# Fused cross-attention stage: a LayerNorm shift moved from VectorE to GpSimd, and the statistics that follow it moved half a step

## The chip, the cores and the metric

One core of one Trainium2 chip runs the whole program. The metric is the device time of one execution in microseconds (us). Engines are named PE (TensorE), DVE (VectorE), ACT (ScalarE), POOL (GpSimd) and SP (the queue that issues most plain DMAs).

## The reference, cut to what matters

Two blocks follow each other on 128 x 64 = 8192 tokens of width 128, 16 heads of 8. The first is self attention, cross attention and a mixture of 8 experts (top 2), each followed by a LayerNorm. The second is a pre-norm cross attention and an MLP. The change lies where the two meet:

```python
# end of block 0 (y: tokens after cross attention)
x  = _layernorm(y + _moe(y, ...), ln3_g, ln3_b)       # third LayerNorm: scale, gain g, shift b
# start of block 1
qn = _layer_norm(x, ln1_g, ln1_b)                      # the "next" LayerNorm, of the new tokens x
Q  = (qn @ wq + bq)                                    # K, V from the context
x  = x + softmax(Q K^T / sqrt(8)) V @ wo + bo
x  = x + gelu(_layer_norm(x, ln2_g, ln2_b) @ w1 + b1) @ w2 + b2
```

## The kernel before, in words

The program runs five parts one after the other: constants, the first block's two attentions, the routing, the experts (their output rows go to DRAM), and `fused_phase` with the final MLP behind it. Only `fused_phase` (L1280) is touched.

`fused_phase` works on 16 groups of 512 tokens (a tile of 128 partitions x 4 x 128). Every engine has its own queue, and its order is written out by hand in a function `step(a)` of that engine; step g works on several groups at once. With g as the group whose attention is in hand (two "quads" of scores, 2g and 2g+1, each as two halves):

- POOL (L1881), step g: `front_rstd(g+2)` (L1865: four tiny instructions that make the reciprocal deviation and the bias of two LayerNorms at once, the own one of group g+2 and the next one of group g+1), the last three of the eight indirect fetches of the expert rows of group g+3 (`fetch`, L1857), `spread(2g-2)` (L1827), `fetch_open(g+4)`, `add_bias(g-1)` (L1834), three fetches of g+4, `spread(2g-1)`, two more fetches of g+4.
- DVE (L1781), step g: `subtract`, `weigh_first(g+3)` (L1720), `maximum`, `recip(2g-1)` (L1685), `weigh_second(g+3)` (L1729), `subtract`, `own_statistics(g+3)` (L1749), `normalise(g-1)` (L1691), `front_moments(g+3)` (L1765), two `maximum` and two `subtract` of quad 2g+2, `recip(2g)`, `gain_own(g+3)` (L1738), `residual(g-1)`, `shift_own(g+3)` (L1743), `maximum`, `next_statistics(g+3)` (L1756), `normalise(g)`.
- ACT (L1636), step g: among exponents and copies, `scale_own(g+2)` (L1615, makes z3) and `scale_next(g+1)` (L1621, makes z4); both wait for `fnb_ready` of POOL.
- PE (L1497): the matmuls and transposes of attention, with `turn_z(g+1)` (L1491), `widen` (L1458, waits for `spread`) and `values` (L1436).

`front_moments(g+3)` aggregates the statistics of the own LayerNorm of group g+3 (written by `own_statistics(g+3)`) together with those of the next LayerNorm of group g+2 (written by `next_statistics(g+2)`), and one semaphore, `fmv_ready`, hands both to POOL. In the kernel before, `next_statistics(g+3)` stands near the end of step g and is used in step g+1. The new tokens `held(a)` lie in `x3`, which has a place for every group. `shift_own` waits for `zg3_ready`, `next_statistics` for `x3_ready`; POOL's `add_bias` also waits for `x3_ready` of a group four steps older than the one made in that step.

The fetches exist for groups up to 15, so POOL issues five of them in steps up to 11 and three up to 12; the first steps (-4 to -1) only fill the pipeline.

Of the kernel before, what the change touches and what calls it, by code (L numbers as in the profile page):

```python
# [7 lines left out]
ALU = mybir.AluOpType  # L8
# [3 lines left out]
P = 128  # L12
D = 128
# [6 lines left out]
GP = GT // P  # L20
# [1259 lines left out]
def fused_phase(nc, c, r, tag, layer, x2_src, rows, final):  # L1280
# [5 lines left out]
    with ExitStack() as ctx:  # L1286
# [33 lines left out]
        zg3 = n.sb("zg3", [P, 2, GP, D])  # L1320
# [28 lines left out]
        def held(a):  # L1349
            return x3[:, bass.ds(a.place, 1)].rearrange("p o t d -> p (o t) d")  # L1350
# [7 lines left out]
        with nc.Block() as block:  # L1358
# [311 lines left out]
            def _(dve):  # L1670
# [20 lines left out]
                def normalise(a, h):  # L1691
                    quad = a.g * 2 + h
                    dve.wait_ge(r_ready, quad + 1)
                    if beyond(a.g, 0):
                        dve.wait_ge(o_ready, a.g)
                    dve.wait_ge(ov_ready, quad + 1)
                    dve.tensor_tensor(ot[:, GT // 2 * h:GT // 2 * h + GT // 2], ps_o[:, GT // 2:GT], ov[:, h, :],
                                      ALU.mult).then_inc(ot_ready, 1)
# [41 lines left out]
                    dve.tensor_tensor(zg3[:, a.u], z3[:, a.u], c.row["ln3_g"][:, None, :].broadcast_to([P, GP, D]),  # L1740
                                      ALU.mult).then_inc(zg3_ready, 1)

                def shift_own(a):  # L1743

                    dve.wait_ge(zg3_ready, a.g + 1)
                    dve.tensor_tensor(held(a), zg3[:, a.u], c.row["ln3_b"][:, None, :].broadcast_to([P, GP, D]),  # L1746
                                      ALU.add).then_inc(x3_ready, 1)

                def own_statistics(a):  # L1749

                    dve.wait_ge(fy_ready, a.g + 1)
# [29 lines left out]
                def step(a):  # L1781
                    if a.unrolled and a.g == NG:
                        final.dve_part(dve, True)
                    g = a.g
                    if a.exists():
                        subtract(g * 2 + 1, 0)
                    if a.shift(3).exists():
                        weigh_first(a.shift(3))
                    if a.exists():
                        maximum(g * 2 + 1, 1)  # L1790
                    if a.shift(-1).exists():
                        recip(g * 2 - 1, 1)
                    if a.shift(3).exists():
                        weigh_second(a.shift(3))
                    if a.exists():
                        subtract(g * 2 + 1, 1)
                    if a.shift(3).exists():
                        own_statistics(a.shift(3))
                    if a.shift(-1).exists():
                        normalise(a.shift(-1), 1)  # L1800
                    if a.shift(3).exists() or a.shift(2).exists():
                        front_moments(a.shift(3))
                    if a.shift(1).exists():
                        maximum(g * 2 + 2, 0)
                        maximum(g * 2 + 2, 1)
                        subtract(g * 2 + 2, 0)
                        subtract(g * 2 + 2, 1)
                    if a.exists():
                        recip(g * 2, 0)
                    if a.shift(3).exists():  # L1810
                        gain_own(a.shift(3))
                    if a.shift(-1).exists():
                        residual(a.shift(-1))
                    if a.shift(3).exists():
                        shift_own(a.shift(3))
                    if a.shift(1).exists():
                        maximum(g * 2 + 3, 0)
                    if a.shift(3).exists():
                        next_statistics(a.shift(3))
                    if a.exists():  # L1820
                        normalise(a, 0)
                over_steps(dve, step, NG - 4)
# [3 lines left out]
            def _(pool):  # L1826
# [30 lines left out]
                def fetch(a, first, end):  # L1857
                    for i in range(first, end):
# [3 lines left out]
                            in_offset=bass.IndirectOffsetOnAxis(ap=sl[:, a.u, choice, t:t + 1], axis=0)).then_inc(  # L1862
                                yg_in[a.u], 16)

                def front_rstd(a):  # L1865
                    pool.wait_ge(fmv_ready, a.g + 1)
                    if beyond(a.g, 1):
                        pool.wait_ge(z3_ready, a.g - 1)
                    if beyond(a.g, 2):
                        pool.wait_ge(fz_ready, a.g - 2)  # L1870
                    pool.tensor_tensor(fneg[:, a.u, :], fmv[:, a.u, :, 0], c.minus_one[:, 0:2 * GP], ALU.mult)
                    pool.tensor_tensor(frstd[:, a.u, :], fmv[:, a.u, :, 1], c.eps[:, 0:2 * GP],
                                       ALU.add).then_inc(fvar_ready, 1)
                    pool.wait_ge(fvar_ready, a.g + 1)
                    pool.tensor_tensor(frstd[:, a.u, :], frstd[:, a.u, :], c.minus_half[:, 0:2 * GP],  # L1875
                                       ALU.pow).then_inc(frstd_ready, 1)
                    pool.wait_ge(frstd_ready, a.g + 1)
                    pool.tensor_tensor(fnb[:, a.u, :], fneg[:, a.u, :], frstd[:, a.u, :], ALU.mult).then_inc(
                        fnb_ready, 1)

                def step(a):  # L1881
# [18 lines left out]
                        spread(g * 2 - 1, 1)  # L1900
                    if a.shift(4).exists():
                        fetch(a.shift(4), 3, 4)
                        fetch(a.shift(4), 4, 5)
                pool.wait_ge(bob_ready, 1)
                over_steps(pool, step, NG - 4)
# [502 lines left out]
```

## Time and profile before

| | us |
|---|---|
| median of 3 runs | 1475.5 |
| lowest and highest | 1467.96 and 1479.77 |
| span of the profiled execution, first to last instruction | 1416.2 |
| median less that span (what lies around it) | 59.3 |
| fused stage in the profile, from the first fetch to the last residual add | about 949 to 1284 |

The profiled execution has no separate time of its own, so the median less the span is taken for what lies around the span. Times in rows are us from the span's start. Instruction durations overlap a little at their edges; what counts in a queue is the distance from one start to the next.

### The profile page before, as it was taken

Reading aid. Unit: us, or ns where it says so; the run is one execution under the profiler, and the core shown is the slowest. Engines: PE = TensorE matmul, PEld = TensorE weight load, DVE = VectorE, ACT = ScalarE, POOL = GpSimd, SP = SyncE. Lnnn points to the kernel's source line nnn. Section 1 sums busy time; section 2 is a strip of 40 time slices with the busy share of each in tenths; the row PEclk is TensorE's granted clock in tenths of the full one; section 3 lists DMA queues with packets and bytes.
Section 4 is the critical chain, followed back from the end, with each engine's and each line's share of the span. In section 5 each row is a group of like instructions: output and inputs, shape, how many; then the busy total and the mean of one; then the engine's idle time right before and its main releaser. Section 6 shows DMA issues by size and latency. Waiting matters only on the chain. (4 is left out here: it accounts for less than half of the span.)

```text
span 1416.2 us, 59902 instructions
## 1 busy us (share of the span) xinstructions
PE 1253.1 (88%) x23136; PEld 1052.9 (74%) x23136; DVE 962.8 (68%) x2123; ACT 993.5 (70%) x2030; POOL 866.3 (61%) x1340
## 2 busy tenths in 40 slices
PE   4999999989999998668899999961699999998997
PEld 2778877777888887657899999960577777785775
DVE  3777777767787875588455555534799999963331
ACT  1777777767888885298566666641789999974553
POOL 1567667666766774310899999848677777423331
PEclk9999999999999998559899999985799999999999
DMA  3233323323232242052222222222233333121221
GB/s 108 70 94 93 111 90 96 99 85 91 82 89 81 81 129 76 8 183 70 61 67 69 68 67 70 65 62 65 76 90 92 92 94 91 52 61 53 71 70 45
DMA packets 140281, 113.91 MB, mean 80 GB/s; under 512 B 17184, under 2 KB 113952, under 8 KB 140192
## 3 DMA queue, kind: packets, MB, share of 16 engines
q1 hardware_dynamic: 131744, 95.42, 22.9%
q0 software_dynamic: 8448, 17.32, 4.9%
q8 instruction: 54, 0.88, 0.3%
q14 instruction: 35, 0.29, 0.1%
HBM read 78.55 MB, written 34.08 MB: 80 GB/s over the span
## 5 line engine op out<-in xcount | busy, mean ns | idle before, releaser
L832 DVE TENSOR_REDUCE at_mx<-at_ps_s 128x16 f32<-128x1024 f32 x128 | 156.1, 1220 | 106.8 <-PE at_ps_s L561 60.7
L761 ACT ACTIVATE at_pt<-at_ps_t 128x1024 f32<-128x1024 f32 x128 | 130.6, 1020 | 56.3 <-PE at_ps_t L575 55.4
L2225 POOL DMA_INDIRECT ex_xg<-x,ex_ti x136 | 148.0, 1088 | 23.3 <-issue 21.9
L754 ACT ACTIVATE at_pr<-at_dd 128x1024 f32<-128x1024 f32 x128 | 135.2, 1056 | 34.7 <-DVE at_dd L840 34.6
L2306 DVE COPY ex_wt<-experts 128x1156 f32 x136 | 104.8, 772 | 75.7 <-DVE ex_y L2312 72.9
L2285 ACT ACTIVATE ex_hg<-ex_ps_h,ex_wt 128x128 f32<-128x128 f32 x544 | 154.4, 372 | 1.3 <-PE ex_ps_y L2254 1.2
L840 DVE TENSOR_TENSOR at_dd<-at_ps_s,at_mx 128x1024 f32<-128x1024 f32 x128 | 153.7, 1202 | 0.1
L1860 POOL DMA_INDIRECT l_yg<-rows,l_sl x128 | 128.9, 1007 | 33.8 <-issue 30.5
L2245 PE MATMUL ex_ps_h<-ex_xt,ex_wt 128*128 128x128 f32 x1088 | 147.2, 279 | 0.0
L575 PE MATMUL at_ps_t<-ident,at_pr 128*128 128x128 f32 x1024 | 139.9, 280 | 5.2 <-issue 4.2
L2254 PE MATMUL ex_ps_y<-ex_wt,ex_hg 128*128 128x128 f32 x1088 | 143.7, 275 | 0.7 <-ACT ex_hg L2285 0.7
L962 POOL TENSOR_TENSOR at_rcx<-at_rc,own 128x256 f32<-128x256 f32 x64 | 39.2, 613 | 159.9 <-DVE at_rc L848 159.9
L2245 PEld LDWEIGHTS ex_ps_h<-ex_xt,ex_wt 128*128 128x128 f32 x1088 | 133.3, 193 | 2.7
L2254 PEld LDWEIGHTS ex_ps_y<-ex_wt,ex_hg 128*128 128x128 f32 x1088 | 132.3, 192 | 1.1 <-ACT ex_hg L2285 1.1
L575 PEld LDWEIGHTS at_ps_t<-ident,at_pr 128*128 128x128 f32 x1024 | 113.5, 142 | 23.2 <-issue 15.3
L589 PE MATMUL at_ps_o<-at_pt,vx 128*32 128x64 f32 x4096 | 123.7, 222 | 5.3 <-issue 3.4
L594 PE MATMUL at_ps_o<-at_pt,count 128*32 128x64 f32 x4096 | 122.6, 221 | 6.3 <-issue 6.2
L589 PEld LDWEIGHTS at_ps_o<-at_pt,vx 128*32 128x32 f32 x4096 | 95.5, 111 | 32.8 <-ACT at_pt L761 22.0
L594 PEld LDWEIGHTS at_ps_o<-at_pt,count 128*32 128x32 f32 x4096 | 97.8, 111 | 7.0 <-issue 7.0
L2277 ACT ACTIVATE ex_xt<-ex_ps_x 128x128 f32<-128x128 f32 x136 | 37.7, 277 | 91.8 <-PE ex_ps_x L2237 82.6
L1130 PEld LDWEIGHTS l_ps_s<-mlp_w,mlp_hid 128*128 128x128 f32 x512 | 67.1, 191 | 31.7 <-issue 29.6
L953 POOL TENSOR_TENSOR at_qb<-at_qt,side 128x256 f32<-128x256 f32 x128 | 74.5, 613 | 24.7 <-ACT at_qt L734 19.1
(240 smaller groups left out, 3174.9 us busy)
## 6 DMA issues: line engine op xcount, KB each, us to landing
rows<-ex_y SPq DMA_DIRECT2D x136, 64.0 KB
x<-at_ln_out SPq DMA_DIRECT2D x32, 256.0 KB, 3.2
at_kx<-in_xt SPq DMA_DIRECT2D x16, 256.0 KB, 2.8
at_qx<-in_xt SPq DMA_DIRECT2D x16, 256.0 KB, 2.8
at_vin<-in_xt SPq DMA_DIRECT2D x16, 256.0 KB, 2.7
at_xr<-in_x SPq DMA_DIRECT2D x16, 256.0 KB, 2.9
x1t<-at_xt SPq DMA_DIRECT2D x16, 256.0 KB, 3.3
at_kx<-in_ctxt SPq DMA_DIRECT2D x16, 256.0 KB, 2.8
```

What stands on the lines that cost most here:

```text
L575: tr = pe.transpose(ps_t[:, b, r, :], pr[:, p, r, 2 * b:2 * b + 2, :], c.ident[:, :])
L589: pe.matmul(ps_o[32 * r:32 * r + 32, SEQ * b:SEQ * b + SEQ], c.vx[:, 0, QB * h + b, r, 24 * f:24 * f + 32], pt[:, 2 * h + b // 2, b % 2, r ...
L594: mm = pe.matmul(ps_o[32 * r:32 * r + 32, GT // 2:GT // 2 + SEQ], c.count[:, b, f, :], pt[:, 2 * h + b // 2, b % 2, r, SEQ * f:SEQ * f + SEQ],
L754: act.activation(pr[:, p], dd[:, p], ACT.Exp, scale=SCALE).then_inc(p_ready, 1)
L761: act.activation(pt[:, 2 * h + p], ps_t[:, :, :, :], ACT.Copy).then_inc(pt_ready, 1)
L832: dve.tensor_reduce(mx[:, p], ps_s[:, :, 4 * p:4 * p + 4, :], AX.X, ALU.max).then_inc(mx_ready, 1)
L840: dve.tensor_tensor(dd[:, p], ps_s[:, :, 4 * p:4 * p + 4, :], mx[:, p, :, :, None].broadcast_to([P, 4, 4, SEQ]), ALU.subtract).then_inc(d_ ...
L1860: pool.indirect_dma_start(out=yg[:, a.u, choice, t, :], out_offset=None, in_=rows, in_offset=bass.IndirectOffsetOnAxis(ap=sl[:, a.u, choic ...
L2225: pool.indirect_dma_start(out=xg[:, s, :], out_offset=None, in_=x_src, in_offset=bass.IndirectOffsetOnAxis(ap=ti[:, s:s + 1], axis=0)).the ...
L2245: mm = pe.matmul(ps_h[s % HB][:, f, :], wt[:, s % HB, W1 + P * f:W1 + P * f + P], xt[:, s % HB, :], start=True, stop=True)
L2254: mm = pe.matmul(ps_y[s % 2][:, :], hg[:, s % 2, f, :], wt[:, s % HB, W2 + D * f:W2 + D * f + D], start=(f == 0), stop=(f == FC - 1))
L2285: ins = act.activation(hg[:, s % 2, f, :], ps_h[s % HB][:, f, :], ACT.Gelu, bias=wt[:, s % HB, B1 + f:B1 + f + 1])
```

## The change

`shift_own` becomes a POOL instruction. It stands in POOL's step g, for group g+2, between the fourth and the fifth fetch of group g+4. `next_statistics` moves on DVE from the end of step g (for group g+3) to the middle of step g+1, directly before `front_moments`, and so, written for step g, works on group g+2.

```diff
 DVE, functions
-                def shift_own(a):
-
-                    dve.wait_ge(zg3_ready, a.g + 1)
-                    dve.tensor_tensor(held(a), zg3[:, a.u], c.row["ln3_b"][:, None, :].broadcast_to([P, GP, D]),
-                                      ALU.add).then_inc(x3_ready, 1)
-
 DVE, step
                     if a.shift(-1).exists():
                         normalise(a.shift(-1), 1)
+                    if a.shift(2).exists():
+                        next_statistics(a.shift(2))
                     if a.shift(3).exists() or a.shift(2).exists():
                         front_moments(a.shift(3))
...
                     if a.shift(-1).exists():
                         residual(a.shift(-1))
-                    if a.shift(3).exists():
-                        shift_own(a.shift(3))
                     if a.shift(1).exists():
                         maximum(g * 2 + 3, 0)
-                    if a.shift(3).exists():
-                        next_statistics(a.shift(3))
                     if a.exists():
                         normalise(a, 0)
 POOL, functions
+                def shift_own(a):
+
+                    pool.wait_ge(zg3_ready, a.g + 1)
+                    pool.tensor_tensor(held(a), zg3[:, a.u], c.row["ln3_b"][:, None, :].broadcast_to([P, GP, D]),
+                                      ALU.add).then_inc(x3_ready, 1)
 POOL, step
                         spread(g * 2 - 1, 1)
                     if a.shift(4).exists():
                         fetch(a.shift(4), 3, 4)
+                    if a.shift(2).exists():
+                        shift_own(a.shift(2))
+                    if a.shift(4).exists():
                         fetch(a.shift(4), 4, 5)
```

## Rows read from the trace of the kernel before

**Rows 1.** Busy us by stretch: length, then PE, PEld, DVE, ACT, POOL, clock, DMA

```profile
1031.40:1205.00 173.60, 160.09 (x4041) 128.36 (x4042) 172.83 (x410) 157.96 (x252) 136.53 (x170) 1.00 0.34 91
1205.00:1222.30 17.30, 15.91 (x405) 12.76 (x406) 17.20 (x41) 15.73 (x26) 8.37 (x10) 1.00 0.21 59
1222.30:1237.80 15.50, 14.14 (x357) 11.10 (x359) 14.68 (x25) 14.05 (x23) 5.01 (x7) 1.00 0.17 49
```

**Rows 2.** Timeline of POOL, one steady step; start, us, operation, [idle time before it]

```profile
1118.23 0.20 POOL L1871 TENSOR_TENSOR l_fneg<-l_fmv,minus_one 128x8 f32<-128x8 f32 x1 [1.12 <-DVE l_fmv L1778]
...
1123.39 1.14 POOL L1860 DMA_INDIRECT l_yg<-rows,l_sl  x1 [0.30 <-DVE l_rc L1689]
1124.56 1.01 POOL L1831 TENSOR_TENSOR l_rcx<-l_rc,own 128x256 f32<-128x256 f32 x1
...
1125.95 1.28 POOL L1838 TENSOR_TENSOR l_xb<-l_x,l_bob 128x512 f32<-128x512 f32 x1
...
1131.29 0.75 POOL L1831 TENSOR_TENSOR l_rcx<-l_rc,own 128x256 f32<-128x256 f32 x1 [0.22 <-DVE l_rc L1689]
1132.18 0.99 POOL L1860 DMA_INDIRECT l_yg<-rows,l_sl  x1 [0.15 <-issue]
...
1135.53 0.20 POOL L1871 TENSOR_TENSOR l_fneg<-l_fmv,minus_one 128x8 f32<-128x8 f32 x1 [1.11 <-DVE l_fmv L1778]
```

**Rows 3.** Timeline of ACT, the same step: its z4 copy, and its two waits

```profile
1125.87 0.58 ACT L1632 ACTIVATE l_qx<-l_ps_g 128x512 f32<-128x512 f32 x1
...
1128.23 1.45 ACT L1570 ACTIVATE l_qb<-l_ps_g,l_side,side 128x512 f32<-128x512 f32 x2 [0.83 <-PE l_ps_g L1471]
...
1131.21 0.38 ACT L1606 ACTIVATE l_ov<-l_ps_o 128x256 f32<-128x256 f32 x1 [0.61 <-issue]
```

**Rows 4.** Timeline of DVE, the same step

```profile
1124.23 0.87 DVE L1746 TENSOR_TENSOR l_x<-l_zg,const_rows 128x512 f32 x1
1125.02 1.21 DVE L1673 TENSOR_REDUCE l_mx<-l_ps_s 128x16 f32<-128x1024 f32 x1
1126.16 0.28 DVE L1762 BATCH_NORM_STATS2 l_fstats<-l_x 128x6 f32 x1
...
1126.37 0.66 DVE L1762 BATCH_NORM_STATS2 l_fstats<-l_x 128x6 f32 x3
1126.95 0.40 DVE L1697 TENSOR_TENSOR l_ot<-l_ps_o,l_ov 128x256 f32<-128x256 f32 x1
...
1134.68 0.17 DVE L1778 BATCH_NORM_AGGREGATE l_fmv<-l_fstats 128x2 f32<-128x6 f32 x1
...
1134.77 0.54 DVE L1778 BATCH_NORM_AGGREGATE l_fmv<-l_fstats 128x2 f32<-128x6 f32 x7
```

**Rows 5.** Durations in ns (least, median, most) of three lines over the run

```profile
L1831 POOL TENSOR_TENSOR l_rcx<-l_rc,own x32: 612/744/1029, 1018.4 to 1280.1; 128x256 f32<-128x256 f32 x32
L1860 POOL DMA_INDIRECT l_yg<-rows,l_sl x128: 940/980/1341, 949.4 to 1210.2; - x128
L1746 DVE TENSOR_TENSOR l_x<-l_zg,const_rows x16: 691/873/1735, 970.8 to 1228.5; 128x512 f32<-128x512 f32 x8, 128x512 f32 x8
```

**Rows 6.** Timeline of PE: the query projection, and the key projection behind `values`

```profile
1127.09 1.02 PE L1471 MATMUL l_ps_g<-l_qx,mats 128*128 128x512 f32 x2
...
1130.10 1.12 PE L1466 MATMUL l_ps_g<-l_kx,mats 128*128 128x512 f32 x2
```

**Rows 7.** Timeline of POOL while the pipeline fills, and at its first wait

```profile
979.09 0.21 POOL L1871 TENSOR_TENSOR l_fneg<-l_fmv,minus_one 128x8 f32<-128x8 f32 x1
...
1011.90 0.20 POOL L1871 TENSOR_TENSOR l_fneg<-l_fmv,minus_one 128x8 f32<-128x8 f32 x1 [6.63 <-DVE l_fmv L1778]
```

**Rows 8.** Timeline where the shift (DVE) meets `add_bias` (POOL), last group

```profile
1228.48 1.74 DVE L1746 TENSOR_TENSOR l_x<-l_zg,const_rows 128x512 f32<-128x512 f32 x1
...
1228.40 1.27 POOL L1838 TENSOR_TENSOR l_xb<-l_x,l_bob 128x512 f32<-128x512 f32 x1
```

**Rows 9.** Timeline of POOL: the one late fetch of the ten steady steps

```profile
1181.74 0.94 POOL L1860 DMA_INDIRECT l_yg<-rows,l_sl  x1 [1.40 <-issue]
```

## The prediction, made before the changed kernel ran

> **What bounds the kernel now.** I read the busy time by stretch first, then the timelines of POOL, ACT and DVE over one step, then the chain that ended last, to see where the stage hangs outside its steady part. The fused stage runs ten steps between 1031.4 and 1205.0 (that is where POOL's `front_rstd` starts), 17.36 us each [rows 1]; an undisturbed one takes 17.30 (1118.23 to 1135.53 [rows 2]). In this stretch DVE is busy 172.8 of 173.6 us, PE 160.1, ACT 158.0 [rows 1]: DVE has no gap and sets the step. POOL's 136.5 us look light, but its queue is not. Between two fetches lie 0.30 us that nothing fills, and the only real gaps of its step are 0.22 us before the second `spread` and 1.11 before `front_rstd`, which waits for DVE's moments [rows 2]: 1.3 us of slack a step. ACT has gaps of 0.83 and 0.61 [rows 3].
>
> **What is taken from DVE.** The shift of 512 columns: from its start to the next one's, 1125.02 - 1124.23 = 0.79 us a step [rows 4]. The statistics only change place (1126.16 to 1126.95, another 0.79). DVE's own work falls to 17.3 - 0.8 = 16.5 us a step. If nothing else bound, ten steps would give back 8 us.
>
> **What is given to POOL.** One add of 128x512 with a broadcast row. POOL does the same shape in `add_bias`, 1.28 us [rows 2]. The gap of 0.30 between two fetches gives way to the smaller ones around a tensor instruction (0.03 before, 0.15 behind, as round the spreads), so POOL's step grows by 1.2 us against 1.3 of slack. By occupation alone it just fits.
>
> **What the new order closes.** `front_moments` on DVE now stands behind `next_statistics`, which waits for POOL's shift, which stands behind the second `spread` and a fetch; and POOL's next step begins with `front_rstd`, which waits for those moments. That is a loop of one step through the whole POOL queue. Its length from `front_rstd` on, in durations of before:
> - 1118.23 to 1131.07, where POOL is free for the second `spread` (1131.29 less its wait of 0.22) [rows 2]: 12.84;
> - `spread` 0.75, gap 0.15, fetch 0.99 [rows 2]: 14.7;
> - 0.05 and the shift 1.28 [rows 2]: 16.1;
> - POOL's semaphore to DVE, 0.12, an estimate between 0 and the 0.22 that DVE's takes to POOL;
> - four statistics 0.87 (1126.16 to 1127.03), 0.04, eight moments 0.63 (1134.68 to 1135.31) [rows 4]: 1.54;
> - 0.22 back to POOL (1135.31 to 1135.53) [rows 2, 4].
>
> Together 17.95 us. Off it comes what POOL loses to DVE today. The first `spread` takes 1.01 where it begins while DVE's shift runs (1124.23 to 1125.10) [rows 2, 4]; with the shift gone I take the least of its line, 0.61 [rows 5], so 0.4 off. The fetch at 1123.39 takes 1.14 [rows 2] against a median of 0.98 [rows 5]; 0.1 off. The second `spread` no longer starts right on DVE's `recip`, in `weigh_second`, because 1.6 us of DVE work (shift and statistics) leave the stretch before it; 0.1 off. That makes 17.35. DVE needs 16.5 and waits some 0.1 to 0.9 us for the shift.
>
> A second loop runs through ACT and PE. ACT's z4 copy ends 8.4 us after the moments (1126.45 less 1118.01 [rows 3]); PE's query projection and `values` take 3.0 (1127.09 to 1130.10 [rows 6]); then 0.1 and `recip` 0.6, 0.15 and `spread` 0.61, 0.15 and fetch 0.99, shift 1.33, 0.12, 1.54: 17.0. It doesn't decide, but is near. ACT gets its bias up to 1.7 us later behind DVE's `subtract`, since statistics and wait now stand between that and the moments; its gaps of 0.83 and 0.61 [rows 3] give way, as projection and `recip` come no later than before.
>
> So a steady step costs 17.35 for 17.30: ten of them +0.5 us. Bounds: 16.5 (POOL's fetches and gaps shrink beside a lighter DVE) and 17.95 (no contention is won back), so -8 and +6.5.
>
> **Filling the pipeline.** From 949 to 981 the chain that ended last runs through POOL alone: fetch after fetch, then `front_rstd`, which shows no wait before it at 979.09 [rows 7]. Step -2 now holds the shift of group 0 (1.2 us more), and behind it POOL does one fetch (1.1) while DVE needs 0.12 + 1.54 + 0.22: 0.8 of waiting. So the first z4, and with it all attention, starts 2.0 us later. Step -1 loses as much again, but there the chain runs through PE and DVE, and POOL has 6.63 us of wait at 1011.90 [rows 7]: nothing. Between 0 and +2.5, I take +2.0.
>
> **Draining it.** From step 12 on POOL is light (8.4 us busy of 17.3 [rows 1]), so the shift is early and DVE's gain shows: 0.7 us in step 12. In the next stretch the last shift took 1.74 us [rows 8], as it met `add_bias`; with it gone PE, 14.1 of 15.5 us busy [rows 1], lets about 0.8 through. Together -1.5; between 0 and -2.5.
>
> **The hiccup.** Once in the ten steps a fetch came 1.1 us late (1.40 before it, not 0.30 [rows 9]), and POOL's slack took most of it. Without slack: +0.7.
>
> **The sum.** +0.5 + 2.0 - 1.5 + 0.7 = +1.7 us on a span of 1416.2; with the 59.3 us around it 1477. The runs of before lie between 1468.0 and 1479.8, so their median of 1475.5 may itself be off by a few us.
>
> **A rule of the skill, weighed.** DVE's shift takes 691, 873 and 1735 ns (least, median, most) [rows 5]. The longest began beside `add_bias`, which ran to 1229.67, and ended 0.55 us behind it [rows 8]: it stood still while POOL ran. The Trainium skill (SBUF — State Buffer, its single rule on the shared port pair) says that a DVE instruction with two SBUF inputs and a GpSimd instruction that reads SBUF exclude each other for the whole instruction, and the one that comes second pays; by that rule, the trace agrees. It is the ground for the first rival below.
>
> **The rivals.**
> - *POOL's instructions meet DVE's two-input ones (slower).* DVE reaches `weigh_first` 1.6 us earlier than before, about 8.8 us behind the moments, which is where `add_bias` ends if `spread` is shortened; and the second `spread` still lies in `weigh_second`. If they block each other, DVE or POOL loses up to 0.6 us a step, as the shift's 0.87 to 1.74 over 0.69 shows [rows 5, 8]; it decides once it eats the 0.1 us of wait that my loop leaves DVE. With 17.95 a step: +6.5 + 2.0 - 1.5 + 0.7 = +8, 1483. With 0.6 more, 1489. For it: the pair in [rows 8]. Against it: the shift itself falls on statistics and on reads of PSUM.
> - *DVE's saving comes through (faster).* If POOL closes its loop in 16.5, the step is DVE's: -8 + 2.0 - 1.5 = -7.5, 1468. For it: DVE alone has no gap [rows 1]. Against it: the median fetch (0.98) is already near the least (0.94) [rows 5], and 0.8 would have to come from there.
> - *ACT's gaps don't give way.* Then its later bias is added, 0.8 to 1.3 us a step: +10 to +14, 1486 to 1490. Against it: what both gaps wait for comes earlier now.
>
> **How the numbers follow.** A measurement tells about 1% (15 us) from no change. Forecast (step 17.2 to 17.6): 0.60, 1475 to 1481. Meeting or contention not won back: 0.18, 1482 to 1489. ACT: 0.05. DVE's saving: 0.17, 1466 to 1472. Hardly any of these passes 15 us; with a few us of spread between runs, slower by over 1% gets 0.09, faster 0.05, within 1% 0.86. The range that leaves out 2 in 10 is 1467 to 1486.
>
> **What would show it.** Right: POOL's `front_rstd` starts 17.2 to 17.6 us apart; the gap before it is 0.6 to 0.9 us, not 1.11; DVE has a gap of 0.1 to 0.9 before `next_statistics`, released by POOL's shift; the first `spread` takes about 0.6; the z4 of group 0 is 2 us later; ACT waits for the bias, with smaller gaps elsewhere. Wrong: steps of 16.6 with DVE still gapless, a much longer `weigh_first` or `add_bias`, or ACT keeping both its gaps. A median outside 1467 to 1486 would be wrong as a whole.

## The result, and the profile after

| us | before | after | ratio, 95% interval |
|---|---|---|---|
| first set of runs (4 and 4) | 1474.3 (1468.0 to 1479.8) | 1455.9 (1452.0 to 1458.1) | 0.9873 [0.9846, 0.9900] |
| same kernel again, second set | 1474.1 | 1457.9 | 0.9880 [0.9827, 0.9932] |
| same kernel again, fifth set | 1418.7 | 1427.4 | 1.0058 [1.0035, 1.0082] |

The change made the kernel 18 us faster, where 1.7 us slower was forecast and 1467 was the lower end of the range. But the third row says that this is only half of the answer. A set here is a group of kernels that ran together on one chip, each with the kernel before beside it. In six sets the kernel before took 1474.3, 1474.1, 1474.7, 1419.0, 1418.7 and 1475.0 us: two values 56 us apart, no single run between 1428.2 and 1465.6, and always one value among the timed runs of a set. In two sets at 1474 the change gains 1.3 and 1.2%, in one at 1419 it costs 0.6%. So there are two questions: what the 56 us are, and what the change does with and without them.

The profiled execution of after, from the first set, took 1456.8 us:

```profile
core 0: 1454.1 us, clock 0.940
```

So 2.7 us lie around the span. For the kernel before, 59.3 us had been put there. A profile of the kernel before taken in the second set settles it: time 1473.8, span 1471.1, the same 2.7 us. The profile that stands ahead of the prediction was taken in an execution of the 1419 kind (span 1416.2), and the times beside it were of the 1474 kind; whether it ran together with them is not on record. The missing 55 us were not around the span. By the starts of `front_rstd` 3.3 us of them lie before the ten steady steps, 47.4 in these and 4.2 behind.

Busy us in ten steady steps, each time from one `front_rstd` to the tenth after it (columns as in [rows 1]: length, PE, PEld, DVE, ACT, POOL, clock, DMA share and GB/s): first the kernel before in a 1474 set, then after in a 1474 set, then after in a 1419 set.

```profile
1034.70:1255.70 221.00, 187.14 (x4038) 145.13 (x4038) 173.14 (x410) 161.54 (x251) 135.39 (x170) 0.95 0.26 72
```

```profile
1040.20:1241.50 201.30, 170.36 (x4044) 130.94 (x4042) 166.03 (x401) 158.79 (x251) 143.59 (x180) 1.00 0.29 79
```

```profile
1032.00:1212.60 180.60, 162.10 (x4049) 127.37 (x4052) 166.67 (x401) 158.32 (x251) 143.17 (x181) 1.00 0.32 88
```

Against [rows 1] (173.60 us) the work of DVE is nearly the same: 173 us in the kernel before in both kinds, 6 to 7 less in after, which lacks the shift. What differs is the length in which it lies: 22.1, 20.1, 18.1 and, for the kernel before in a 1419 set, 17.4 us a step. In the first row DVE idles 48 us. What it waits for stands in its timeline; after, 1474 set:

```profile
1111.00 1.22 DVE L1673 TENSOR_REDUCE l_mx<-l_ps_s 128x16 f32<-128x1024 f32 x1
1114.67 0.56 DVE L1689 RECIPROCAL l_rc<-l_ps_o 128x64 f32<-128x64 f32 x1 [2.45 <-PE l_ps_o L1452]
```

L1452 is the end of the value product `values`: 128 small pairs of weight load and matmul. Alone it takes 1.83 us. The weight loads of one such product of the kernel before in a 1474 set:

```profile
1125.85 0.16 PEld L1447 LDWEIGHTS l_ps_o<-l_pt,vx 128*32 128x32 f32 x8 [0.16 <-issue]
...
1127.84 0.12 PEld L1447 LDWEIGHTS l_ps_o<-l_pt,vx 128*32 128x32 f32 x2 [0.35 <-issue]
1128.54 0.17 PEld L1447 LDWEIGHTS l_ps_o<-l_pt,vx 128*32 128x32 f32 x4 [0.58 <-issue]
1129.30 0.11 PEld L1447 LDWEIGHTS l_ps_o<-l_pt,vx 128*32 128x32 f32 x1 [0.59 <-issue]
...
1130.02 0.18 PEld L1452 LDWEIGHTS l_ps_o<-l_pt,count 128*32 128x32 f32 x4 [0.55 <-issue]
1130.75 0.52 PEld L1487 LDWEIGHTS l_ps_g<-mats,l_ot 128*128 128x128 f32 x4 [0.55 <-issue]
```

TensorE does a few pairs, then stands still for 0.55 to 0.6 us with nothing that releases it ("issue"), and again. Beside it POOL's queue runs three fetches:

```profile
1124.70 0.20 POOL L1871 TENSOR_TENSOR l_fneg<-l_fmv,minus_one 128x8 f32<-128x8 f32 x1 [1.11 <-DVE l_fmv L1778]
...
1127.26 1.03 POOL L1860 DMA_INDIRECT l_yg<-rows,l_sl  x1 [0.16 <-issue]
1128.59 0.95 POOL L1860 DMA_INDIRECT l_yg<-rows,l_sl  x1 [0.30 <-issue]
1129.85 0.94 POOL L1860 DMA_INDIRECT l_yg<-rows,l_sl  x1 [0.31 <-issue]
```

The first gap in the loads opens 0.2 us after the first of them begins. This is what I call the standstill. Two lines measure it for the whole stage, the answers for L1452's weight loads in the profile ahead of the prediction and in the second set (idle us before its loads, times):

```profile
L1452 PEld LDWEIGHTS l_ps_o<-l_pt,count x2048: 106/110/110, 1014.2 to 1279.1; 128*32 128x32 f32 x187
...
  issue: 2.7, 2
```

```profile
L1452 PEld LDWEIGHTS l_ps_o<-l_pt,count x2048: 105/110/178, 1016.1 to 1334.9; 128*32 128x32 f32 x187
...
  issue: 24.2, 45
```

After has 15.2 us in 29 gaps in the 1474 set and 1.9 in one gap in the 1419 set. In the steady steps of the 1419 sets a product beside two or three fetches takes 1.8 to 2.1 us, in those of the 1474 sets mostly 3.0 to 6.2, and a product beside none takes 1.83 to 1.86 in both.

Which products are hit, in the 1474 sets: a step has two, `values(a,0)` about when `front_rstd` runs, and `values(a-1,1)` about when the first three fetches of g+4 run. In the kernel before the first stands still in all of the ten steady steps (3.7 to 5.8 us), the second in seven of them (2.7 to 5.3; 1.9 to 2.1 in the others). After has only the second left; its two products of one step, weight loads and POOL:

```profile
1100.29 0.16 PEld L1447 LDWEIGHTS l_ps_o<-l_pt,vx 128*32 128x32 f32 x8 [0.17 <-issue]
...
1101.94 0.19 PEld L1452 LDWEIGHTS l_ps_o<-l_pt,count 128*32 128x32 f32 x8
...
1111.84 0.11 PEld L1452 LDWEIGHTS l_ps_o<-l_pt,count 128*32 128x32 f32 x1 [0.60 <-issue]
...
1112.55 0.17 PEld L1447 LDWEIGHTS l_ps_o<-l_pt,vx 128*32 128x32 f32 x6 [0.56 <-issue]
1113.29 0.18 PEld L1452 LDWEIGHTS l_ps_o<-l_pt,count 128*32 128x32 f32 x7 [0.57 <-issue]
```

```profile
1100.35 0.21 POOL L1869 TENSOR_TENSOR l_fneg<-l_fmv,minus_one 128x8 f32<-128x8 f32 x1 [0.80 <-DVE l_fmv L1772]
...
1102.91 1.03 POOL L1852 DMA_INDIRECT l_yg<-rows,l_sl  x1 [0.16 <-issue]
...
1109.04 1.03 POOL L1852 DMA_INDIRECT l_yg<-rows,l_sl  x1
1110.38 1.00 POOL L1852 DMA_INDIRECT l_yg<-rows,l_sl  x1 [0.30 <-issue]
1111.68 0.94 POOL L1852 DMA_INDIRECT l_yg<-rows,l_sl  x1 [0.30 <-issue]
1115.39 0.74 POOL L1823 TENSOR_TENSOR l_rcx<-l_rc,own 128x256 f32<-128x256 f32 x1 [2.76 <-DVE l_rc L1689]
...
1117.29 1.29 POOL L1860 TENSOR_TENSOR l_x<-l_zg,const_rows 128x512 f32 x1
```

The first product runs from 1100.29 to 1102.12, beside `front_rstd`, and is over 0.8 us before the next fetch: with the statistics ahead of the moments, the moments, `front_rstd` and the three fetches behind it come later against PE. The second product, from 1110.09, meets the last two of three fetches (the first ended at 1110.07) and ends at 1114.38, 4.3 us for 1.8. Its last gap closes at 1113.29, 0.7 us after the last fetch has left POOL.

TensorE's granted clock has a part in it too. In the first of the three rows above it is 0.95 over the ten steps, in the other two 1.00: in the kernel before, five of the ten steps show 0.86 to 0.93, which is to say that the clock stood at the lower of its two levels (1.2 GHz for 2.4) for some of the step. A step at 1.00 and the longest one, both of the kernel before in the second set:

```profile
1056.10:1077.40 21.30, 17.81 (x410) 13.79 (x406) 17.35 (x41) 16.40 (x27) 13.56 (x18) 1.00 0.27 75
...
1099.70:1124.70 25.00, 20.96 (x420) 16.38 (x413) 17.60 (x41) 16.30 (x26) 13.46 (x18) 0.86 0.24 63
```

The five steps at 1.00 take 21.2 to 21.5 us, the five others 21.4 to 25.0, together 7.4 us more. As an estimate from these steps, up to 7.4 of the 19.7 us that the change takes off the ten steps went with the drops of the clock, and the rest with the standstill alone. In after and in stats_only, where only the second product stands still, no steady step shows a drop.

Where the 17.0 us between the spans of the two kernels went (1471.1 and 1454.1, by the starts of `front_rstd`): the ten steps -19.7, filling the pipeline +5.5 (1040.2 for 1034.7), from there to the end -2.8.

### The profile page after: what moved, and what is told of

It reads as the page before. It is cut to its first block and busy times, and to the rows that moved or that the text cites. A ratio compares the mean times of both kernels' runs of the same rounds, so it can differ in the third digit from the quotient of the medians.

```text
span 1454.1 us, 59906 instructions
## 1 busy us (share of the span) xinstructions
PE 1269.1 (87%) x23136; PEld 1059.8 (73%) x23136; DVE 951.4 (65%) x2107; ACT 995.2 (68%) x2030; POOL 878.9 (60%) x1356
## 5 line engine op out<-in xcount | busy, mean ns | idle before, releaser
L1852 POOL DMA_INDIRECT l_yg<-rows,l_sl x128 | 125.9, 983 | 31.8 <-issue 29.4
L1673 DVE TENSOR_REDUCE l_mx<-l_ps_s 128x16 f32<-128x1024 f32 x64 | 76.3, 1213 | 25.8 <-PE l_ps_s L1412 20.8
```

Of the source, the lines that this page charges most:

```text
L1852: pool.indirect_dma_start(out=yg[:, a.u, choice, t, :], out_offset=None, in_=rows, in_offset=bass.IndirectOffsetOnAxis(ap=sl[:, a.u, choic ...
```

## The experiments

The theory at the start: the gain is the statistics' place, because it lets one product a step escape the fetches. Rivals: it is DVE's relief, by the shift on POOL; or the two kernels differ for a reason that has nothing to do with the order. The kernel before beside each kernel belongs to the same set.

**Both kernels again (second set).** No edit.

> The kernel before, unchanged, profiled once more beside its own timed runs. The profile of before has a span of 1416 us under a median of 1475, that of after a span of 1454 under 1456. Theory A (the profile of before was of an execution that its timed runs are not like): the span comes out at 1465 to 1477, a steady step of the fused stage takes 20 to 21 us in place of 17.3, and TensorE stands still for about 3 us in its value products, as it does in after. Rival B (the timed runs have 59 us outside the span): span 1416 again, time 1475. Ratio to before 1.00 in both.

1475.2, ratio 1.0004 [0.9979, 1.0029]; span 1471.1.

> The kernel after, unchanged. Theory A: span about 1454, time about 1456, ratio 0.987, steps of 20.1 us with the same standstill of TensorE. Rival C (either kernel falls into the state with or without standstill by chance): one of the runs comes out near 1420.

1457.9, 0.9880 [0.9827, 0.9932]. The gain repeats, and so does the span of the kernel before: its first profile is the one that stands apart.

**The two halves of the change (second set).**

```diff
# stats_only: the statistics move, the shift stays on DVE
+                    if a.shift(2).exists():
+                        next_statistics(a.shift(2))
                     if a.shift(3).exists() or a.shift(2).exists():
                         front_moments(a.shift(3))
...
-                    if a.shift(3).exists():
-                        next_statistics(a.shift(3))
```

> Only the statistics are moved, the shift stays on VectorE. If the gain of the change lies in the shift leaving VectorE, the ratio is 1.00 (0.997 to 1.004). If it lies in where the statistics stand (they leave the stretch between the first maximum and normalise, so that normalise and the subtraction behind it come 0.8 us earlier), the ratio is 0.987 to 0.993.

1451.8, 0.9844 [0.9789, 0.9898], step 20.5: somewhat more than I had expected of it.

```diff
# shift_only: shift_own on POOL, directly behind the third fetch of its step; statistics in their old place
                         fetch(a.shift(3), 7, 8)
+                    if a.shift(2).exists():
+                        shift_own(a.shift(2))
```

> Only the shift goes to GpSimd, directly behind the third fetch of a step; the statistics stand where they stood. If the gain lies in the shift leaving VectorE, the ratio is 0.987 to 0.993, unless VectorE waits for GpSimd before the statistics (the shift ends there about 7.7 us behind the moments, VectorE comes to the statistics at 7.4, so a wait of 0.3 us). If the gain is that of the statistics' place, the ratio is 1.00 to 1.01.

1485.8, 1.0070 [1.0043, 1.0097], step 23.0. The whole gain is the move of the statistics; the shift on POOL alone, in this place, costs 0.7%. The place is not that of the change: here the shift stands ahead of the first `spread`. With both moved, as in after, the step is 0.4 us shorter than in stats_only (20.1 for 20.5), but the ten steps begin 6.7 us later (1040.2 for 1033.5), so the time is no better.

**No indirect fetch at all (third set).**

```diff
# plain_fetch: eight plain DMAs per group on SP; GpSimd's fetch does nothing
+                    for choice in range(2):
+                        for t in range(GP):
+                            sp.dma_start(yg[:, a.u, choice, t, :], rows[bass.ds(a.place * GT + (choice * GP + t) * P, P), :]).then_inc(yg_in[a.u], 16)
...
-                        pool.indirect_dma_start(
```

> The kernel before, but the expert rows come by plain DMAs of the same size from SP's queue, in order and not gathered, so GpSimd issues no fetch (the output is that of the wrong rows; everything else is computed). Theory P (TensorE's value products, 128 pairs of load and matmul, stand still wherever two or three of GpSimd's indirect fetches run beside them; 1.83 us alone, 3.7 to 5.8 beside fetches): every value product takes 1.8 to 2.0 us, the steady step is 17.0 to 17.5 us instead of 22, the time 1405 to 1425. Rival Q (the standstill is TensorE's own, from its loop or its rate, whatever GpSimd does): the products keep 3.7 to 5 us, time over 1450.

The gather is left out, so the rows are not those of the tokens, at equal bytes. 1406.2, 0.9539 [0.9513, 0.9564]. All the steady products take 1.83 to 1.86 us. `front_rstd` starts 17.1 us apart, and POOL waits for the moments:

```profile
1085.46 0.20 POOL L1869 TENSOR_TENSOR l_fneg<-l_fmv,minus_one 128x8 f32<-128x8 f32 x1 [3.43 <-DVE l_fmv L1781]
...
1102.57 0.20 POOL L1869 TENSOR_TENSOR l_fneg<-l_fmv,minus_one 128x8 f32<-128x8 f32 x1 [3.43 <-DVE l_fmv L1781]
```

The same bytes in the same stage, by plain DMAs, hold nothing up. So it is the indirect fetches on GpSimd, not the amount of their traffic. Whether it is their issue on GpSimd, the queue that they go through or the scattered rows is not separated: the plain DMAs read rows that follow each other. (Part of the time is a faster fill, as the fetches filled it.)

**GpSimd waits for the first product (third set).**

```diff
# before_wait: the kernel before with
                         front_rstd(a.shift(2))
+                    if a.shift(-1).exists():
+                        pool.wait_ge(pv_ready, g * 2 - 1)
+                        tick(0)
```

> The kernel before, only that GpSimd waits for the first value product of the step (quad 2g-2) before its three first fetches (with a tiny instruction that carries the wait). The statistics stay where they were. Theory P, by which the change gains because it starts these fetches only after that product: the products of the first quad take 1.8 us, the second ones keep 4.2, the step is 20 to 20.7 us, the time 1450 to 1460 (ratio 0.984 to 0.990). If the gain has to do with VectorE's order itself: 1470 to 1485.

1455.4, 0.9860 [0.9833, 0.9888], step 20.5, first product 1.83 us in each step, second 4.3 to 5.6, once 1.86. The granted clock over the ten steps is 0.98 for 0.95 in the kernel before of the second set. This is the test of the mechanism: DVE's order isn't touched, no work is taken away, a wait and a tiny instruction are added, and the time falls as far as with the change.

**The second product freed instead (third set).** Four fetches behind the second `spread`, one before `add_bias`.

```diff
# stats_apart (on stats_only) and before_apart (on the kernel before)
+                        fetch(a.shift(4), 0, 1)
...
                         add_bias(a.shift(-1))
-                        fetch(a.shift(4), 0, 1)
-                        fetch(a.shift(4), 1, 2)
-                        fetch(a.shift(4), 2, 3)
...
                         spread(g * 2 - 1, 1)
+                        fetch(a.shift(4), 1, 2)
+                        fetch(a.shift(4), 2, 3)
```

> Statistics moved as in the change, shift on VectorE, and GpSimd's fetches taken out of the second value product as well: in step g it does one fetch of group g+4, add_bias, the second spread and then the other four. Theory P: both value products near 1.9 us, step 17.4 to 18.2 us, time 1420 to 1432. Rival Q: 1450 or more. If the four fetches at the end of the step reach into the next first product, it is that one that takes 3 to 4 us, and the time 1435 to 1450.

1493.4, 1.0133 [1.0105, 1.0161], step 23.8.

> The same order of GpSimd's fetches on the kernel before, with the statistics in their old place. Theory P: the second product is free of fetches, the first one meets the three fetches of the next group as before where the moments come early; step 18 to 21 us, time 1430 to 1462, slower than stats_apart. Rival Q: 1470 to 1480.

1498.2, 1.0151 [1.0123, 1.0180], step 24.5. Both are misses of mine. The second product is free (1.83 to 1.86), but in the steady steps POOL of stats_apart no longer waits before `front_rstd`, and the three fetches behind that meet the first product, which runs from 1130.80 to 1136.92, 6.1 us:

```profile
1127.25 0.94 POOL L1860 DMA_INDIRECT l_yg<-rows,l_sl  x1 [0.30 <-issue]
1128.21 0.21 POOL L1871 TENSOR_TENSOR l_fneg<-l_fmv,minus_one 128x8 f32<-128x8 f32 x1
...
1130.77 1.03 POOL L1860 DMA_INDIRECT l_yg<-rows,l_sl  x1 [0.16 <-issue]
1132.11 0.96 POOL L1860 DMA_INDIRECT l_yg<-rows,l_sl  x1 [0.30 <-issue]
1133.37 0.94 POOL L1860 DMA_INDIRECT l_yg<-rows,l_sl  x1 [0.30 <-issue]
1138.01 0.84 POOL L1831 TENSOR_TENSOR l_rcx<-l_rc,own 128x256 f32<-128x256 f32 x1 [3.69 <-DVE l_rc L1689]
```

Two more things add to the loss. The four fetches now run beside the scores (L1412, 32 loads), and these stand still as well; of stats_apart:

```profile
1127.69 0.20 PEld L1412 LDWEIGHTS l_ps_s<-l_kb,l_qb 32*128 32x128 f32 x2 [0.52 <-issue]
1129.10 0.55 PEld L1412 LDWEIGHTS l_ps_s<-l_kb,l_qb 32*128 32x128 f32 x11 [1.21 <-issue]
```

In the ten steps such gaps before L1412's loads add up to 21.3 us, in the kernel before to 3.9. So it is not the value products alone that can be hit. And the granted clock is 0.86 over the ten steps of stats_apart and 0.88 over those of before_apart, for 0.95 in the kernel before.

**Both products freed (fourth set).** stats_wait is stats_only with the wait of before_wait. The two others have that wait and POOL's fetches split into two ahead of `add_bias` and three behind the second `spread`, on stats_only and on the kernel before:

```diff
# stats_two_three and before_two_three
                         fetch_open(a.shift(4))
                         fetch(a.shift(4), 0, 1)
                         fetch(a.shift(4), 1, 2)
                         add_bias(a.shift(-1))
                         spread(g * 2 - 1, 1)
                         fetch(a.shift(4), 2, 3)
                         fetch(a.shift(4), 3, 4)
                         fetch(a.shift(4), 4, 5)
```

> A control for the theory that the statistics' move gains only because it lets the first value product of a step run before GpSimd's fetches. With the statistics moved and the shift left on VectorE that product already runs free (1.83 us) in every step, so GpSimd's explicit wait for it should change nothing: 1450 to 1455 us, step 20.4 to 20.6, first product 1.83 us and second 4.5 as there. If the wait itself were what gained in the kernel before (by holding GpSimd back for some other reason), it should gain again here, about 15 us: 1435 to 1440.

1432.3 for 1419.0, 1.0086 [1.0067, 1.0106], step 18.3.

> Statistics moved, GpSimd waits for the first product, and the early fetches of group g+4 are split: two behind the first spread, then add_bias and the second spread, then three. By the standstill theory both value products of a step now run beside no fetch or only the edge of one (1.83 to 2.5 us each), and the step falls to 17.5 to 19 us, so 1415 to 1435 us. By the rival (any order in which GpSimd has more to do between the second spread and the next moments loses, as the two kernels with four fetches there did) the step is 21 to 24 us and the time 1460 to 1495. In between, 1440 to 1455: one product is still hit, and the trace says which.

1439.3 for 1419.0, 1.0116 [1.0082, 1.0149], step 19.2.

> The same wait and the same split of the fetches, with the statistics where they stood before. If the standstill beside fetches is all that separates the kernels, the place of the statistics matters no more once both products are free: same time as its companion with the statistics moved, within 5 us. If the statistics' move has a gain of its own, this one is slower by 10 us or more. And if it is below 1440, the kernel before was held up by GpSimd's order alone.

1427.2 for 1419.0, 1.0048 [1.0031, 1.0065], step 18.4.

The set was one without the standstill (the kernel before 1419.0; products beside three fetches 2.0 to 2.1 us), so what these three were made for was not tested. They showed two other things. The order that frees products costs something by itself: even stats_wait, whose wait holds nothing back here, takes 18.3 us a step, as the statistics' move alone does in the fifth set. And in before_two_three, where `add_bias` was moved beside `weigh_first`, DVE's four instructions took 2.52 us for 1.12 in the kernel before, 1.4 us more, where the step grew by 1.0; the kernel before, then DVE and POOL of before_two_three:

```profile
1128.40 1.12 DVE L1725 SCALAR_TENSOR_TENSOR l_y<-l_yg,l_wt,l_fx 128x128 f32<-128x128 f32 x4
```

```profile
1098.31 2.52 DVE L1725 SCALAR_TENSOR_TENSOR l_y<-l_yg,l_wt,l_fx 128x128 f32<-128x128 f32 x4
```

```profile
1098.57 1.31 POOL L1838 TENSOR_TENSOR l_xb<-l_x,l_bob 128x512 f32<-128x512 f32 x1
```

**The change and its halves again (fifth set).** The same three kernels as after, stats_only and shift_only, sent because of what the fourth set showed.

> In the last set of runs the kernel before took 1419 us and its value products did not stand still, as in the profile that the prediction was made from; in the sets before it took 1474 and they did. So the change has two effects to be told apart. If this set is one without the standstill: the prediction's own sum says before + 1.7 (1421 for 1419, steps 17.35). The rival, from the trace with the statistics moved and GpSimd waiting (steps 18.3 without any standstill): the loop moments - front_rstd - z4 - attention - next moments is longer than I summed, and the changed kernel is slower than before here, 1427 to 1437 for 1419. If the set is one with the standstill: 1456 for 1474 again, as in two sets.

1427.4 for 1418.7, 1.0058 [1.0035, 1.0082], step 18.1.

> Statistics moved, shift left on VectorE. Without the standstill: by the sum of the prediction VectorE stays full and the step 17.3 to 17.4, so before + 0 to 2 us; by the rival about 18.3 a step as with GpSimd's wait added, 1428 to 1434 for 1419. With the standstill: 1452 for 1474 again.

1428.3, 1.0051 [1.0029, 1.0072], step 18.3.

> Only the shift on GpSimd, statistics in their old place. Without the standstill: GpSimd has 1.3 us of slack a step and gains 1.2 us of work, VectorE loses 0.8, so the step is between 16.5 and 17.5: before - 8 to + 2. If GpSimd turns out to be what bounds, 17.6 to 18: before + 3 to + 8. With the standstill: 1486 for 1474 again.

1429.2, 1.0064 [1.0040, 1.0089], step 18.5.

Without the standstill all three are slower. shift_again is slower than either of my ranges for it. Its shift delays the first `spread`, which starts 7.7 us behind `front_rstd` (1093.43 less 1085.75) for 6.3 in [rows 2], and TensorE's `widen` waits for that `spread`. I take this for the reason; no run tests it.

Why the changed kernel is slower is read from the trace of a_third. ACT, then DVE:

```profile
1088.53 1.65 ACT L1611 ACTIVATE l_z<-l_fy,l_fnb,l_frstd 128x128 f32<-128x128 f32 x4 [0.84 <-POOL l_fnb L1876]
...
1093.73 0.58 ACT L1632 ACTIVATE l_qx<-l_ps_g 128x512 f32<-128x512 f32 x1
...
1096.02 1.45 ACT L1570 ACTIVATE l_qb<-l_ps_g,l_side,side 128x512 f32<-128x512 f32 x2 [0.76 <-PE l_ps_g L1471]
...
1098.88 0.38 ACT L1606 ACTIVATE l_ov<-l_ps_o 128x256 f32<-128x256 f32 x1 [0.50 <-issue]
```

```profile
1085.36 0.64 DVE L1772 BATCH_NORM_AGGREGATE l_fmv<-l_fstats 128x2 f32<-128x6 f32 x8
...
1098.24 0.56 DVE L1689 RECIPROCAL l_rc<-l_ps_o 128x64 f32<-128x64 f32 x1 [0.67 <-PE l_ps_o L1452]
...
1102.35 0.28 DVE L1756 BATCH_NORM_STATS2 l_fstats<-l_x 128x6 f32 x1
...
1103.33 0.64 DVE L1772 BATCH_NORM_AGGREGATE l_fmv<-l_fstats 128x2 f32<-128x6 f32 x8
```

Read as a loop of four engines, the step is: from the end of the moments (1086.00) through `front_rstd`, z3 and z4 to the end of the copy of z4 (1094.31) 8.31 us; projection and second value product until `recip` starts (1098.24) 3.93; `recip`, `weigh_second`, subtract, own statistics, normalise, next statistics and moments (to 1103.97) 5.73. Together 17.97. The sum equals the step whatever bounds it, as it runs from the end of one step's moments to the end of the next step's; what speaks for this chain is that it is followed through waits that end just before the next link (POOL's 0.80 for the moments, ACT's 0.84 for the bias, DVE's 0.67 for the product) and through DVE's queue without a gap. In the profile ahead of the prediction the same three stretches run from 1118.01 over 1126.45 (the copy of z4 [rows 3]) and 1130.58 to 1135.31 [rows 4]; its DVE:

```profile
1117.47 0.54 DVE L1778 BATCH_NORM_AGGREGATE l_fmv<-l_fstats 128x2 f32<-128x6 f32 x7
...
1130.58 0.54 DVE L1689 RECIPROCAL l_rc<-l_ps_o 128x64 f32<-128x64 f32 x1
```

They are 8.44, 4.13 and 4.73, together 17.30. The last stretch has grown by 1.00, and the statistics are 0.98 of it (1102.35 to 1103.33). POOL's shift was not what closed the loop: it ended at 1102.14, and DVE reached the statistics at 1102.35 without a gap.

**The loop made shorter (sixth set).** VectorE's `subtract(2g+1, 1)` behind `front_moments`, in three kernels, and the shift alone in another place:

```diff
# after_early (on after), before_early (on before), late_early (on shift_late)
-                    if a.exists():
-                        subtract(g * 2 + 1, 1)
...
                         front_moments(a.shift(3))
+                    if a.exists():
+                        subtract(g * 2 + 1, 1)
# shift_late: POOL's shift directly behind the first spread; next_statistics(g+3) last in DVE's step
```

> Theory for a set without the standstill (before 1419, after 1427, step 18.1): the step is a loop of three engines. Moments - front_rstd - z3 and z4 - their copy (8.3 us), query projection and second value product to recip (3.9), recip to the next moments on VectorE (5.7, of which 0.9 are the statistics that the change put there). Here VectorE's subtract of quad 2g+1 (1.2 us) goes from inside that last stretch to behind the moments. The loop falls to about 16.9 and VectorE's own work (16.5) or GpSimd's queue (about 17.2) is next: step 16.9 to 17.4, 1412 to 1420. Rival (GpSimd's queue through the shift sets the step, as the prediction's first loop had it): no gain, 1425 to 1430, since that loop holds no subtract. With the standstill: it is whatever lets a product run before the fetches; 1440 to 1475.

1499.5 for 1475.0, 1.0178 [1.0145, 1.0211], step 23.4.

> Shift on GpSimd directly behind the first spread, statistics at the end of VectorE's step behind normalise, so outside the loop and without a wait for the shift. By the loop theory, without the standstill: 17.2 to 17.5 a step, since the loop of the kernel before (17.30) never held the shift; 1415 to 1422 for 1419. If instead VectorE's occupation bound the kernel before, the 0.8 us taken from it come through: 16.5 a step, 1410. With the standstill: both products are hit as in the kernel before, 1470 to 1485 for 1474.

1485.9, 1.0084 [1.0060, 1.0108], step 22.6.

> The last kernel with the subtract behind the moments too: loop 16.1, VectorE 16.5, GpSimd 17.1 or so (16.3 busy and the gaps of its waits). Without the standstill: 16.6 to 17.2 a step, 1408 to 1416, faster than the kernel before and the best of all. With it: 1450 to 1480.

1485.8, 1.0077 [1.0050, 1.0104], step 22.9.

> The kernel before with only the subtract behind the moments. VectorE keeps its full 17.3 us of work, so without the standstill nothing is gained by the shorter loop: 1416 to 1421 for 1419. If it gains more than 5 us, VectorE's gapless timeline was overlap of starts and not work; if it loses, the later subtract holds up ScalarE's exponent. With the standstill: the moments come 1.2 us earlier, both products stay hit, 1465 to 1480.

1482.7, 1.0049 [1.0032, 1.0066], step 22.6.

The set was one with the standstill, so what these kernels were to show of the loop stays untested. All four came out slower than the ranges that I had given for such a set, shift_late by a little. In after_early the moved `subtract` holds TensorE up: the scores of the next quad are written over what it reads (`ps_s`), and wait for it. These scores in after (1474 set), with no wait, then in after_early:

```profile
1118.30 0.98 PEld L1412 LDWEIGHTS l_ps_s<-l_kb,l_qb 32*128 32x128 f32 x32
```

```profile
1109.18 1.80 PEld L1412 LDWEIGHTS l_ps_s<-l_kb,l_qb 32*128 32x128 f32 x32 [3.57 <-DVE l_dd L1681]
```

Over the ten steps TensorE's waits for a `subtract` ahead of its scores grow from 5.9 to 29.2 us, and DVE's for the scores from 10.2 to 30.8. The first product no longer ends before the fetches (3.2 to 4.6 us; the second takes 3.1 to 3.9), which adds less than 1 us a step to the two together, and the granted clock is 0.91 for 1.00. So all that the change had gained (0.987) is lost and more (1.018), and that wait is the largest thing that is new. before_early and late_early have it too, at 12.1 and 11.9 us.

## Why the prediction was wrong

**The step that failed: what bounds the kernel.** "DVE has no gap and sets the step" was read from a profile whose span lay 59 us under the median of the times, and the difference was written off as lying around the span. It lay inside: in the runs that were timed DVE idled 48 of 221 us: 28.8 of them `recip` waited for L1452, the end of value products that stood still beside fetches (15 waits; 39.0 us in 20 over the whole stage), and 15.3 went to waits for the scores, which stand behind the products in TensorE's queue. All other terms were worked out for an execution that the timed runs were not. The sign was in the table: a span of 1416.2 against a lowest time of 1468.0. None of my rivals held a kernel that waits for PE, so the range could not hold 1456.

**By the steps, in the execution they were made for.** The fifth set gives what the sum meant to say (span 1423.9 for 1416.2, +7.7 us). Slower was right there, at under a quarter of the size and by another path than the one that I named:

| term | predicted | measured |
|---|---|---|
| ten steps and the hiccup | +1.2 | +7.0 (180.6 for 173.6) |
| filling | +2.0 | +0.6 (1032.0 for 1031.4) |
| draining | -1.5 | +0.1 |
| sum | +1.7 | +7.7 |

- *The loop through POOL (17.35)* was well sized in its parts: the shift took 1.28 us, and POOL had 0.80 to 0.93 us before `front_rstd`, where I gave 0.6 to 0.9. The first `spread` took 0.62 for a predicted 0.61. But it didn't decide.
- *The loop through ACT and PE (17.0, "It doesn't decide, but is near")* is, as the trace of a_third reads, the one that does, and it was mis-sized by 0.9 us (the sixth set, made to test it, was of the other kind). I added 8.4 us up to the end of the z4 copy (1126.45 [rows 3]) and 3.0 us from the projection's start (1127.09 [rows 6]), and left out the 0.64 us between the two; 0.57 of it is there in a_third. TensorE does eight transposes (L1433) in it, which stand ahead of the projection in its queue and wait for an ACT copy behind z4. `recip` begins 0.36 us behind the product, not 0.1. And behind `recip` I took POOL's way to the shift, though DVE's own queue up to the statistics is as long (4.11 us, the shift 3.90).
- *"Its gaps of 0.83 and 0.61 give way"* was wrong: they are 0.76 and 0.50, and ACT's wait of 0.84 for the bias comes on top. That is the rival to which I gave 0.05, "ACT's gaps don't give way", at 0.8 us a step; measured is 0.7.
- *DVE's gap before the statistics* wasn't there; its time is lost elsewhere, 0.67 us before `recip` and 0.59 before a normalise, both behind PE.
- *POOL meets DVE's two-input instructions*: it did not happen in the changed kernel (`weigh_first` 1.14 us). Where it was made to, in before_two_three, it cost 1.4 us, more than the 0.6 I had allowed. The Trainium skill (SBUF — State Buffer, Who interferes with whom) says that a DVE instruction with two SBUF inputs contends with a GpSimd instruction that reads SBUF, and that the second to issue is blocked until the first is done. By that rule, the trace agrees: the longest of `weigh_first`'s instructions takes 1.99 us for a median of 0.34 beside an `add_bias` of 1.31.

**In the runs that were timed** the same lengthened loop is hidden: the moments come later, the three fetches behind them come after the first product instead of on it, and 2 us a step are won (20.1 for 22.1), up to 0.7 of it by a clock that no longer drops. The shift on POOL takes another 0.4 us off the step and loses more than that in filling the pipeline: stats_only has the longer step (20.5) and the better time.

**What stays open.** Why two or three of GpSimd's indirect fetches stop TensorE's stream of small pairs in some sets and hardly touch it in others: the kernel, the fetches (0.94 to 1.03 us each) and their bytes are the same, and the second and the fourth set, one of either kind, ran on the same chip. The queue of instruction loads does not tell them apart either: three packets in 120 us (1060 to 1180) in the kernel before in both kinds. No kernel was tried that frees both products in a set with the standstill, and none that shortens the loop in a set without it. So no version here is shown to beat both kernels in both kinds of set: stats_only is the best of them with the standstill (1451.8 for 1474.1), the kernel before without it (1418.7).

## What to carry to other kernels

When the span of a profile and the times of the same kernel differ by more than the few us that other profiles of the program show around the span, the profile is of another kind of execution, and nothing may be summed from it until that is explained; here 1.7 to 2.8 us was the true margin and 59 the warning. When a move makes one semaphore later, follow every loop that passes through it, with the gaps between one engine's end and the next one's start written down as terms of their own. And where a dense stream of small matmuls can fall beside indirect fetches, try a wait that orders them before reordering the work: three lines gave what the whole change gave.

## What the runs showed of the hardware that was not expected

- 128 pairs of a 128x32 weight load and a 128x64 matmul take 1.83 us alone and, in sets with the standstill, mostly 3.0 to 6.2 us beside two or three indirect fetches of GpSimd, in pieces of a few pairs with gaps of mostly 0.55 to 0.6 us between them; in the longest ones a part is the lower clock. The scores' loads are hit in the same way (21.3 us in ten steps of stats_apart). Plain DMAs of the same bytes do nothing of the kind (1.83 to 1.86 in all steady products).
- The same program has this in some sets of runs and not in others (1474 and 1419 us), with the same kind in all timed runs of a set.
- The granted clock is lower where both products stand still: 0.95 over the ten steps of the kernel before in a 1474 set and 1.00 in a 1419 set. In the kernels where only the second product stands still it is 1.00 (stats_only, after) and 0.98 (before_wait).
- A wait added to GpSimd made the kernel 1.4% faster (0.9860 [0.9833, 0.9888]).
